# The first score work of each next layer is moved between the last MLP step's products, in a fused four-layer transformer kernel

## The chip, the cores and the metric

The kernel runs on one core of one Trainium2 chip. The metric is the device time of one execution in microseconds (us); lower is better. A core has TensorE (PE in the rows; PEld is its weight load), VectorE (DVE), ScalarE (ACT), GpSimd (POOL) and SyncE, whose queue (SPq) issues most DMAs.

## What is computed

An input x of 32 sequences x 128 tokens x 144 channels goes through four conditioned transformer layers. Each layer normalises, modulates with a shift and a scale made from a condition vector, does attention with 16 heads of 9 dimensions, and an MLP with 576 hidden units:

```python
h = modulate(norm(x), shift_msa, scale_msa)
q, k, v = split(h @ w_qkv + b_qkv)            # 16 heads of 9
# layer 2 alone: q = q / |q| * 3 * qg, k = k / |k| * 3 * kg, each head by itself
attn = softmax(q @ k.T * 9 ** -0.5)
x = x + gate_msa * (attn @ v @ w_proj + b_proj)
h = modulate(norm(x), shift_mlp, scale_mlp)
# layer 0: four experts, top two of them weighted per token; layers 1 to 3: one MLP
x = x + gate_mlp * (gelu(h @ w1 + b1) @ w2 + b2)
```

Layers 0 to 2 attend within a sequence. Layer 3 groups tokens in another way (a head-by-head product for each token), which the kernel gets by masked score tiles of the same size.

## The kernel before, in words

**Tiling.** Everything stays in SBUF as 32 sequences, in 8 groups of 4. Sequence group n of layer l has the number n = 8l + g (so 16 is the first of layer 2, 17 the second). An attention phase works through 64 units of 8 heads of one sequence; U is the running number of a unit over all layers, so group n starts at U = 8n and layer l at U = 64l. An MLP phase has 8 steps g, one for each group.

**One unit of attention.** TensorE makes the scores for the maximum (L650, `scores_for_max`) into banks 0 and 1; VectorE takes the negated maxima (L1546, `head_max`). For two units at a time TensorE turns these (L657, `turn_max`) and VectorE copies them out (L1553, `max_out`, tile mT). Then TensorE makes the scores again, transposed and with the maximum taken off (L668 and L672, `scores`), ScalarE takes the exponential (L1235, `weights`), and TensorE multiplies with V (L684, `weigh`). Outputs are turned back (L692) and divided on VectorE (`normed`, L1562 and L1564). `scores_for_max` runs AHEAD = 5 units before `weigh`.

**How q and k come to be.** While group n is attended to, q and k of group n+2 are projected in three pieces m = 0, 1, 2 (`q_and_k`). ScalarE rounds a piece to bfloat16 (`part1`, L1195), VectorE makes the rest (`rest1`, L1496, tile res), GpSimd makes two further parts (`parts23`, L1962 and L1964). SyncE writes them to DRAM (L417, layer 3: L420) and reads them back in another layout in 12 DMAs (L447, `read_parts`). The first `scores_for_max` of a group waits for all 12. In unit u = 3 of each group TensorE does that of the next group. In layer 2, q and k are first made by token (L613), their squares summed (`head_sums`, L1505), the factor 1/|q| found by three Newton rounds (`head_factors`, L1515 to L1528), and VectorE multiplies (`head_norms`, L1537); then TensorE transposes the pieces (L597). There the three pieces are finished in units u = 3, 4 and 5.

**The rows of the next phases.** Each group is normalised before it is turned (`stats`, `factor`, `normalise` on VectorE: L1472 and L1474, tile xn; `copies` on GpSimd: L1957, tile xr). In the MLP of layer l the groups 0, 1, 2 of the next layer are made ready, too; group 3 of the next layer (numbers k = 35 for layer 2 and 51 for layer 3) is normalised in step 7.

**What sets the order.** Each engine runs one hand-written list; semaphores alone tie the lists together. An engine that waits does nothing behind the wait, and the same holds for SyncE's queue. At a layer's start, `start_layer` on TensorE did five `scores_for_max`, two `turn_max` and the first `scores` in a row (for layer 3 the first five, and for layer 1 as well, stood in the last MLP step already). TensorE's first expert product (L960) waited on one semaphore, `q_w1`, for all four experts' weights.

## Time and profile before

| | |
|---|---|
| median of 3 runs | 1554.76 us (1547.8 to 1559.91) |
| the profiled execution | 1548.05 us, of which the span from first to last instruction is 1546.1 us |
| granted TensorE clock over the span | 0.964 of full |
| layer 0: attention, MLP | 64 to 246 us, 246 to 582 us |
| layer 1: attention, MLP | 583 to 757 us, 758 to 869 us |
| layer 2: attention, MLP | 880 to 1100 us, 1100 to 1219 us |
| layer 3: attention, MLP | 1221 to 1450 us, 1451 to 1546 us |

The span is counted from the first instruction, and every time in the rows is on that scale. The durations and positions are those of the one profiled execution.

### The profile page before, as it was taken

Reading aid. Unit: us, or ns where it says so; the run is one execution under the profiler, and the core shown is the slowest. Engines: PE = TensorE matmul, PEld = TensorE weight load, DVE = VectorE, ACT = ScalarE, POOL = GpSimd, SP = SyncE. Lnnn points to the kernel's source line nnn. Section 1 sums busy time; section 2 is a strip of 40 time slices with the busy share of each in tenths; the row PEclk is TensorE's granted clock in tenths of the full one; section 3 lists DMA queues with packets and bytes.
Section 4 is the critical chain, followed back from the end, with each engine's and each line's share of the span. In section 5 each row is a group of like instructions: output and inputs, shape, how many; then the busy total and the mean of one; then the engine's idle time right before and its main releaser. Section 6 shows DMA issues by size and latency. Waiting matters only on the chain. (4 is left out here: it accounts for less than half of the span.)

```text
span 1546.1 us, 41104 instructions
## 1 busy us (share of the span) xinstructions
PE 1410.9 (91%) x16016; PEld 1055.9 (68%) x16016; DVE 1036.5 (67%) x2601; ACT 779.5 (50%) x1287; POOL 541.6 (35%) x739
## 2 busy tenths in 40 slices
PE   5799988999999998999999688877999799998998
PEld 2377676777777776777777566666776577776776
DVE  4698885666776677888447689897355466665342
ACT  2377664333323336676555366665544365555543
POOL 3355542211131304554323324433335134343222
PEclk9799999999999999999999899999999799999999
DMA  4765631111122123554001333453207576774011
GB/s 129 161 151 155 148 95 52 51 44 44 36 70 70 33 73 87 144 146 120 20 29 46 105 94 92 110 129 86 45 24 108 90 109 114 132 131 93 25 54 47
DMA packets 209129, 134.94 MB, mean 87 GB/s; under 512 B 142461, under 2 KB 191320, under 8 KB 202730
## 3 DMA queue, kind: packets, MB, share of 16 engines
q1 hardware_dynamic: 188978, 129.74, 35.3%
q10 hardware_dynamic: 19960, 2.57, 1.2%
q8 instruction: 130, 2.13, 0.6%
q14 instruction: 61, 0.50, 0.1%
HBM read 98.24 MB, written 33.24 MB: 85 GB/s over the span
## 5 line engine op out<-in xcount | busy, mean ns | idle before, releaser
L1546 DVE TENSOR_REDUCE negm<-banks 128x8 bf16<-128x1024 f32 x256 | 311.0, 1215 | 81.4 <-PE banks L650 79.6
L1235 ACT ACTIVATE prob<-banks 128x1024 f32<-128x1024 f32 x256 | 262.5, 1025 | 191.9 <-PE banks L672 191.1
L1363 ACT ACTIVATE hid<-banks 128x512 f32<-128x512 f32 x144 | 86.0, 597 | 220.3 <-PE banks L961 220.2
L1977 POOL TENSOR_TENSOR X<-X,gx 128x288 f32<-128x288 f32 x128 | 104.1, 826 | 255.0 <-DVE gx L1576 253.2
L977 PEld LDWEIGHTS banks<-wfc,hid 128*128 128x128 f32 x1152 | 156.6, 190 | 29.9 <-issue 20.3
L668 PE MATMUL banks<-qk 54*128 54x128 bf16 (+1 forms) x2048 | 168.7, 236 | 5.3 <-ACT prob L1235 5.0
L672 PE MATMUL banks<-mT,identb 64*128 64x128 bf16 x2048 | 165.7, 225 | 0.9 <-issue 0.9
L977 PE MATMUL banks<-wfc,hid 128*128 128x144 f32 x1152 | 161.1, 286 | 0.0
L650 PE MATMUL banks<-qk 54*128 54x128 bf16 (+1 forms) x2048 | 122.9, 241 | 39.6 <-DVE negm L1546 24.9
L960 PE MATMUL banks<-hT,wfc 128*128 128x512 f32 x288 | 149.6, 601 | 2.4 <-DMA wfc<-in_L_cond_w 2.4
L684 PE MATMUL banks<-prob,V 128*32 128x128 f32 x4096 | 143.5, 282 | 0.0
L1745 DVE TENSOR_TENSOR hid<-hid,qk 128x512 f32<-128x512 f32 x128 | 89.2, 697 | 80.4 <-ACT hid L1363 69.5
L1483 DVE TENSOR_SCALAR hmod<-banks,modr 64x128 f32<-64x128 f32 x256 | 86.8, 396 | 78.2 <-PE banks L583 77.9
L1962 POOL CAST parts<-res 96x512 bf16<-96x512 f32 x96 | 59.0, 615 | 218.7 <-DVE res L1496 217.8
L1388 ACT ACTIVATE hid<-banks 128x512 f32<-128x512 f32 (+1 forms) x120 | 71.1, 596 | 123.0 <-PE banks L951 122.2
L997 PE MATMUL banks<-wfc,hid 128*128 128x144 f32 (+1 forms) x960 | 128.6, 291 | 0.2 <-DVE gx L1576 0.2
L997 PEld LDWEIGHTS banks<-wfc,hid 128*128 128x128 f32 (+1 forms) x960 | 124.4, 194 | 3.9 <-issue 2.7
L650 PEld LDWEIGHTS banks<-qk 54*128 54x128 bf16 (+1 forms) x2048 | 70.0, 102 | 82.0 <-DVE negm L1546 38.2
L950 PE MATMUL banks<-hT,wfc 128*128 128x512 f32 x240 | 124.3, 599 | 0.0
L684 PEld LDWEIGHTS banks<-prob,V 128*32 128x32 f32 x4096 | 107.1, 112 | 16.9 <-issue 6.4
L1178 ACT ACTIVATE hT<-banks,modm 128x128 f32<-128x128 f32 x256 | 99.1, 454 | 34.7 <-PE banks L576 34.6
L961 PE MATMUL banks<-hr,rfc 66*128 66x512 f32 x144 | 115.4, 802 | 0.0
(169 smaller groups left out, 2777.0 us busy)
## 6 DMA issues: line engine op xcount, KB each, us to landing
qk<-qk_scr SPq DMA_DIRECT2D x96, 216.0 KB
gbuf<-gate_scr SPq DMA_DIRECT2D x64, 288.0 KB, 4.5
qk_scr<-parts SPq DMA_DIRECT2D x48, 288.0 KB, 2.8
qk<-qk_scr SPq DMA_DIRECT2D x96, 144.0 KB
qk<-cw_scr SPq DMA_DIRECT2D x8, 1024.0 KB, 4.9
qk_scr<-parts SPq DMA_DIRECT2D x48, 144.0 KB, 2.4
qk<-qk_scr SPq DMA_DIRECT2D x96, 72.0 KB
qk<-tok_scr SPq DMA_DIRECT2D x32, 216.0 KB
```

Source lines behind the costliest of these rows:

```text
L650: mm = pe.matmul(bank[s][:, T * i:T * i + T], operand(l, 0, n, U, s, i), operand(l, 1, n, U, s, i), start=True, stop=True)
L668: pe.matmul(bank[2 + s][:, at], operand(l, 1, n, U, s, i), operand(l, 0, n, U, s, i), start=True, stop=False)
L672: mm = pe.matmul(bank[2 + s][:, at], one_hot(half, 64 * s + 4 * (u % 2) + i, [64, T]), mT[half, u // 2, :], start=False, stop=True)
L684: mm = pe.matmul(bank[4][32 * i:32 * i + 32, T * (2 * s + u % 2):T * (2 * s + u % 2 + 1)], V[:, n % 3, u // 2, VS * h:VS * h + 32], prob[: ...
L950: pe.matmul(bank[2 + i % 2][:], wfc1_t[:, at:at + 128], hT[:, h, :], start=True, stop=False)
L960: pe.matmul(bank[2 + i % 2][:], w, hT[:, h, :], start=True, stop=False)
L961: pe.matmul(bank[2 + i % 2][:], x, hr[:, h, :], start=False, stop=True).then_inc(s_fc1, 1)
L977: mm = pe.matmul(bank[4 + b // 2][:, C * (b % 2):C * (b % 2) + C], hid[:, i % KT, T * b:T * b + T], wfc2[:, e - (t == KT - 1), t, :], star ...
L997: mm = pe.matmul(bank[4 + q][:, C * (b % 2):C * (b % 2) + C], hid[0:rows, t, T * b:T * b + T], wfc2[0:rows, k, t, :], start=(t == 0), stop ...
L1235: act.activation(prob[:, 2 * (U % 3):2 * (U % 3) + 2, :], pairs[1][:], ACT.Exp, scale=scale).then_inc(a_exp, 1)
L1546: dve.tensor_reduce(negm[:, u // 2, :, 4 * (u % 2):4 * (u % 2) + 4], pairs[0][:].rearrange("q s (h k) -> q s h k", k=T), AX.X, ALU.max, ne ...
L1977: pool.tensor_tensor(x, x, gx[:, q, :, :], ALU.add).then_inc(g_x, 1)
```

## The change

Five things change, all by where a step stands in a list, with the same mathematics.

1. **Layer starts.** For layers 1, 2 and 3 the first `turn_max` and the first `scores` move from the layer's start into step 7 of the MLP before, between its products; for layer 2 the first five `scores_for_max` and `head_max` go there too. For layer 3 the first `scores_for_max` stands ahead of the last step's transposes, and so it does for layer 2. VectorE's steps are put in to match: `stats` of group 3 moves to the head of step 7, and its `normalise` moves too (layer 3: to the head of step 7; layer 2: to behind the fifth maximum, the last step of the phase).
2. **Exponential's table.** ScalarE runs a one-element exponential (`exp_table`) behind the last GELU of layers 0, 1 and 2, so that the table is loaded there.
3. **Expert weights.** Each expert's weights have a semaphore, and TensorE waits for an expert's own before its first tile of step 0.
4. **GpSimd scales q and k** of layer 2: `scale_heads` (2 small and 2 large instructions a group) for VectorE's 8 instructions of `head_norms`. Rounds 2 and 3 of `head_factors` now stand together in unit 0.
5. In the expert MLP the last `normed` stands ahead of the first `weighted`.

```diff
-        q_w1 = sem("q_w1")
+        q_w1 = [sem(f"q_w1{e}") for e in range(E)]
@@ tensor: attention, mlp
-                start_layer(l)
+                    if l == 2:
+                        pe.wait_ge(a_qt, CR + 4 * 3)
+                    turn_max(32 * l + 1)
-                    pe.wait_ge(q_w1, 16 * 3 * E)
+                    if g == 0 and t == 0:
+                        pe.wait_ge(q_w1[e], 16 * 3)
+                    if l in (1, 2) and g == 7 and t == 4:
+                        if l == 2:
+                            pe.wait_ge(q_mask, 16 * 12)
+                        scores_for_max(l + 1, U0)
                     if t == 4 and g > 0 and turned_mlp(l, g):
                         turn(turned_mlp(l, g)[0], *before(g))
+                    if l in (1, 2) and g == 7:
                         if b == 0:
+                            scores_for_max(l + 1, U0 + 1)
+                        if b == l % 2 + 1:
+                            first_turn()
+                            scores_for_max(l + 1, U0 + 2)
+                        if b == l % 2 + 2:
+                            scores(l + 1, U0)
+                    if l == 1 and g == 7 and b == 3:
+                        scores_for_max(2, U0 + 3)
+                        if g == 7 and j == NT - 3:
+                            first_turn()
+                        if g == 7 and j == NT - 2:
+                            pe.wait_ge(a_gelu, CR + fc1_base[1])
+                            scores(1, U0)
@@ vector: attention, mlp
-                        if l == 2 and 0 < g < 6 and u <= 1:
-                            head_factors(n + 2, False, (u + 2,))
-                        if l == 2 and g < 6 and 1 <= u <= 2:
-                            head_norms(n + 2, u - 1)
+                        if l == 2 and g < 6 and u == 0:
+                            head_factors(n + 2, False, (2, 3))
                 if l == 1:
+                    head_max(2, U0 + 3)
                     rest1(N + 1, 1, 7)
                     rest1(N + 1, 2, 6)
+                    head_max(2, U0 + 4)
+                    normalise(16 * l + 19)
                     head_sums(N + 2)
-                    head_factors(N + 2)
@@ gpsimd: new, called in units 0 of layer 2's attention and in steps 4 and 6 of layer 1's MLP
+            def scale_heads(n):
+                r = n - 16
+                qs, _ = by_token(n)
+                pool.wait_ge(d_nw, CR + 12 * (r + 1))
+                for side in range(2):
+                    x = rs[:, :, H * side:H * side + H]
+                    pool.tensor_scalar(x, x, gains[:, 2 + side:3 + side], None, ALU.mult).then_inc(g_rg, 1)
+                pool.wait_ge(a_qt, CR + 4 * (r + 1))
+                for side in range(2):
+                    pool.wait_ge(g_rg, CR + 2 * r + side + 1)
+                    v = qs[:, :, C * side:C * side + C].rearrange("t b (d h) -> t b d h", d=D)
+                    pool.tensor_tensor(v, v, rs[:, :, H * side:H * side + H].unsqueeze(2).to_broadcast([T, G, D, H]),
+                                       ALU.mult).then_inc(g_qn, 1)
@@ scalar
+            def exp_table():
+                act.activation(warm[:], mhalf[:, 0:1], ACT.Exp)
```

GpSimd's list at the end of layer 1's MLP is not changed but for the scaling: `copies` of group k = 35 stands ahead of pieces 1 and 2 of group 17 there.

VectorE, from the first statistics of step 7 of layer 1's MLP to layer 2's start. `L1472` is `normalise`, `L1496` `rest1` of group 17, `L1505` the head sums of group 18. Before:

```order
L1455 BN_STATS stat<-X 128x6 x4
L1460 BN_AGGR mv<-stat 128x2 x4
L1496 TENSOR_TENSOR res<-banks,parts 96x512
L1472 TENSOR_SCALAR xn<-X,rstd 128x144 x4
L1576 TENSOR_TENSOR gx<-banks,gbuf 128x288 x2
L1496 TENSOR_TENSOR res<-banks,parts 96x512 x2
L1505 TENSOR_REDUCE ss<-hid 128x32 x4
```

And changed, where `L1569` is `head_max`, `L1530` `rest1`, `L1599` the gate and `L1506` `normalise`:

```order
L1523 SCALAR_TENSOR_TENSOR hr<-hhi,masks,hmod 64x512
L1576 COPY mT<-banks 128x128
L1569 TENSOR_REDUCE negm<-banks 128x2x4
L1530 TENSOR_TENSOR res<-banks,parts 96x512
L1599 TENSOR_TENSOR gx<-banks,gbuf 128x288 x2
L1569 TENSOR_REDUCE negm<-banks 128x2x4
L1530 TENSOR_TENSOR res<-banks,parts 96x512 x2
L1569 TENSOR_REDUCE negm<-banks 128x2x4
L1506 TENSOR_SCALAR xn<-X,rstd 128x144 x4
L1539 TENSOR_REDUCE ss<-hid 128x32 x4
```

The normalisation stood ahead of the last two pieces of group 17 and now stands behind them and behind two more maxima.

GpSimd at the same place, changed (before it is the same but for the line numbers and the two rows that scale, which aren't there). `L1992` copies the row just named, `L2026` adds to X, `L1997` and `L1999` are `parts23` of group 17, and `L2008` and `L2013` scale group 18:

```order
L1992 COPY xr<-xn 128x256
L2026 TENSOR_TENSOR X<-X,gx 128x288 x2
L1997 CAST parts<-res 96x512
L1999 TENSOR_TENSOR parts<-res,parts 96x512
L1997 CAST parts<-res 96x512
L1999 TENSOR_TENSOR parts<-res,parts 96x512
L2008 TENSOR_SCALAR rs<-rs,gains 128x4x16 x2
L2013 TENSOR_TENSOR hid<-hid,rs 128x4x144 x2
```

The parts of group 17 stand behind the copy, so behind the normalisation.

TensorE in step 7 of layer 1's MLP. Before, with `L997` the second products and `L597` the transposes of group 17's q and k:

```order
L951 MATMUL banks<-hr,rfc 128x512
L576 MATMUL banks<-ident,xn 128x128 x4
L583 MATMUL banks<-ident,xr 64x128 x4
L997 MATMUL banks<-wfc,hid 128x144 x20
L597 MATMUL banks<-ident,prob 96x128 x12
```

And changed, where `L651` is `scores_for_max`, `L999` the second products, `L658` `turn_max`, `L669` and `L673` `scores`:

```order
L951 MATMUL banks<-hr,rfc 128x512
L651 MATMUL banks<-qk 128x128 x8
L577 MATMUL banks<-ident,xn 128x128 x4
L584 MATMUL banks<-ident,xr 64x128 x4
L999 MATMUL banks<-wfc,hid 128x144 x5
L651 MATMUL banks<-qk 128x128 x8
L999 MATMUL banks<-wfc,hid 128x144 x10
L658 MATMUL banks<-identb,negm 128x128
L651 MATMUL banks<-qk 128x128 x8
L999 MATMUL banks<-wfc,hid 128x144 x5
L669 MATMUL banks<-qk 128x128 x2
```

The first scores of group 16 now stand ahead of everything else that step 7 has left.

## Rows read from the trace of the kernel before

**Rows 1.** The page's first part: engine, busy us (share of the span), instructions.

```profile
PE 1410.9 (91%) x16016; PEld 1055.9 (68%) x16016; DVE 1036.5 (67%) x2601; ACT 779.5 (50%) x1287; POOL 541.6 (35%) x739
```

**Rows 2.** Stretches: bounds, length, busy us by engine (instructions), clock, DMA share, GB/s.

```profile
578.00:592.00 14.00, 10.20 (x140) 7.84 (x140) 8.56 (x17) 4.95 (x5) 2.08 (x3) 0.88 0.01 1
863.00:903.00 40.00, 24.99 (x264) 19.48 (x264) 28.03 (x62) 15.12 (x29) 10.91 (x17) 0.74 0.27 75
1202.00:1237.00 35.00, 26.24 (x233) 18.75 (x233) 19.11 (x39) 11.31 (x18) 6.72 (x9) 0.73 0.49 87
```

**Rows 3.** Timeline, start of layer 0's MLP: start us, us, instruction xcount [idle before <-releaser].

```profile
246.71 1.13 PE L960 MATMUL banks<-hT,wfc 128*128 128x512 f32 x2 [2.39 <-DMA wfc<-in_L_cond_w]
...
256.40 1.14 PE L977 MATMUL banks<-wfc,hid 128*128 128x144 f32 x8
...
252.81 0.69 DVE L1745 TENSOR_TENSOR hid<-hid,qk 128x512 f32<-128x512 f32 x1 [8.03 <-DMA qk<-cw_scr]
```

**Rows 4.** Timeline, from layer 0's last products to layer 1's start.

```profile
578.36 3.21 PE L977 MATMUL banks<-wfc,hid 128*128 128x144 f32 x24
...
587.40 1.06 PE L583 MATMUL banks<-ident,xr 128*64 128x128 f32 x4
...
584.06 1.28 ACT L1235 ACT_TABLE_LOAD   x1 [6.31 <-PE banks L672]
```

**Rows 5.** Timeline of SyncE's queue: the 12 reads of groups 16, 17, 19, 20, 23.

```profile
849.87 4.23 SPq L447 DMA_DIRECT2D qk<-qk_scr  x12
...
881.23 4.64 SPq L447 DMA_DIRECT2D qk<-qk_scr  x12
...
941.49 4.36 SPq L447 DMA_DIRECT2D qk<-qk_scr  x12
...
970.88 4.45 SPq L447 DMA_DIRECT2D qk<-qk_scr  x12
...
1056.60 4.43 SPq L447 DMA_DIRECT2D qk<-qk_scr  x12
```

**Rows 6.** Timeline of TensorE: first `scores_for_max` of groups 17, 19, 20, 23.

```profile
902.84 0.40 PE L650 MATMUL banks<-qk 54*128 54x128 bf16 x8
...
956.76 0.40 PE L650 MATMUL banks<-qk 54*128 54x128 bf16 x8 [0.70 <-DMA qk<-qk_scr]
...
986.77 0.61 PE L650 MATMUL banks<-qk 54*128 54x128 bf16 x8 [1.21 <-DMA qk<-qk_scr]
...
1071.05 0.61 PE L650 MATMUL banks<-qk 54*128 54x128 bf16 x8 [2.79 <-DMA qk<-qk_scr]
```

**Rows 7.** Timeline, steps 6 and 7 of layer 1's MLP.

```profile
862.78 0.63 PE L576 MATMUL banks<-ident,xn 128*128 128x128 f32 x4 [1.27 <-DVE xn L1472]
...
868.59 1.04 PE L597 MATMUL banks<-ident,prob 128*96 128x128 f32 x8
...
859.49 2.32 DVE L1537 SCALAR_TENSOR_TENSOR prob<-prob,gains,rs 128x144 f32<-128x144 f32 x8
...
870.46 2.15 DVE L1472 TENSOR_SCALAR xn<-X,rstd 128x144 f32<-128x144 f32 x4
...
873.27 1.27 DVE L1496 TENSOR_TENSOR res<-banks,parts 96x512 f32<-96x512 f32 x2
...
877.41 1.16 POOL L1964 TENSOR_TENSOR parts<-res,parts 96x512 bf16<-96x512 f32 x1
```

**Rows 8.** Timeline around layer 3's start.

```profile
1213.20 0.64 PE L650 MATMUL banks<-qk 62*128 62x128 bf16 x8 [3.63 <-DVE negm L1546]
...
1236.91 0.64 PE L650 MATMUL banks<-qk 62*128 62x128 bf16 x8
...
1208.49 5.18 SPq L447 DMA_DIRECT2D qk<-tok_scr  x12
```

**Rows 9.** Lines L1977 and L1948 of GpSimd: ns min/median/max, first and last start, form.

```profile
L1977 POOL TENSOR_TENSOR X<-X,gx x128: 787/795/1285, 101.3 to 1542.5; 128x288 f32<-128x288 f32 x128
...
L1948 POOL TENSOR_SCALAR xn<-X,mv,rstd x100: 842/852/1427, 53.5 to 1451.8; 128x144 f32<-128x144 f32 x100
```

More of the change, by code:

```diff
@@ L593, in q_and_k @@
                 if l == 2:
[L594 removed]
+                    pe.wait_ge(g_qn, CR + 2 * (n - 16) + (2 if m else 1))
                     qs, _ = by_token(n)
@@ L1619, in attention @@
                     dve.wait_ge(d_gate, CR + 2 * m0)
-                for U in range(64 * l, 64 * l + AHEAD):
-                    if l in (0, 2):
-                        head_max(l, U)
-                    if U % 2 == 0 and U > 64 * l:
+                for U in range(AHEAD if l == 0 else 0):
+                    head_max(l, U)
+                    if U in (2, 4):
                         max_out(U // 2 - 1)
+                if l:
+                    max_out(32 * l + 1)
+                if l == 2:
+                    head_factors(n0 + 2, True, (1,))
                 for g in range(8):
@@ L1815, in expert_step @@
                         gated(m0 + g, q, acc[:, 2 * q:2 * q + 2, :])
-                def first_maxima():
-                    for U in range(UNITS * N, UNITS * N + AHEAD):
-                        head_max(l + 1, U)
+                U0 = UNITS * N
                 for g in range(8):
@@ L1831, in mlp @@
                         rest1(N, 2, 6)
+                    if l in (1, 2) and g == 7:
+                        stats(16 * l + 19)
+                        if l == 2:
+                            normalise(16 * l + 19)
+                        head_max(l + 1, U0)
                     for k in turned_mlp(l, g):
                         mod_rem(k, 7)
+                        if l in (1, 2) and g == 7:
+                            head_max(l + 1, U0 + 1)
                         split_rem(k)
-                    for k in prepared_mlp(l, g):
+                    if l in (1, 2) and g == 7:
+                        max_out(U0 // 2)
+                        head_max(l + 1, U0 + 2)
+                    for k in prepared_mlp(l, g) if g < 7 else []:
                         stats(k)
@@ L1842, in mlp @@
                         head_factors(N + (g - 4) // 2)
-                        for side in range(2):
-                            head_norms(N + (g - 4) // 2, side)
                     if l == 1 and g in (5, 7):
                         rest1(N + (g - 5) // 2, 0, 6)
-                    for k in prepared_mlp(l, g):
+                    for k in prepared_mlp(l, g) if g < 7 else []:
                         normalise(k)
@@ L2029, in mlp @@
                         factor(k)
+                    if l == 1 and g in (4, 6):
+                        scale_heads(N + (g - 4) // 2)
                     if g == 0:
```

67 lines of the change are left out of this document (35 added, 32 removed).

## The prediction, made blind

> **What bounds the kernel now.** I read the page's busy shares first: TensorE is busy 91% of the span, VectorE 67% [rows 1]. A change that removes no product can only take from TensorE's idle 9% and from the stretches in which its clock is down. The stretches at the layer boundaries, read next, show where that is [rows 2]: 14 us at the boundary of layers 0 and 1 hold 3.8 us of TensorE idle at a clock of 0.88, 40 us at that of layers 1 and 2 hold 15.0 us at 0.74, 35 us at that of 2 and 3 hold 8.8 us at 0.73. Those are what the first change can reach.
>
> Then the attention phases, by the first score product of each group on TensorE and SyncE's queue beside it. In layer 2 the product waits for the reads of q and k and for nothing else: 0.70, 1.21 and 2.79 us at groups 19, 20 and 23 [rows 6]. The reads' first issue and the product belong together: 941.49 to 956.76, 970.88 to 986.77, 1056.60 to 1071.05, so 15.3, 15.9 and 14.5 us [rows 5, 6]. From the product of one group to the next group's reads pass 14.1 us more (956.76 to 970.88). The two make up the whole period, 30.0 us from group 19 to 20. So attention turns in a ring: product in unit 3, pieces of q and k in units 3 to 5, parts, write, read, next group's product in unit 3. What is taken off elsewhere is given back as a wait at that product, and what makes the ring's first turn late makes the phase late.
>
> **Start of layer 0's MLP.** TensorE starts at 246.71 after 2.39 us of waiting for weights [rows 3]. With expert 0's own semaphore it can start at 244.8, when VectorE has set the row of ones. Two things then stand in the way of the first second-product, at 256.40 before: the divided output, which waited behind VectorE's 8.03 us on the experts' weights per token and now stands ahead of them, and those weights themselves, there at 252.81 as before. VectorE needs 0.69 us: the product can start at about 253.5. Gain 256.40 - 253.5 = **2.9**. If its wait of some 2 us brings the clock down, 1.5.
>
> **Layers 0 to 1.** Before: three second products from 578.36 to 581.6, a turn, mT, the first scores, then 1.28 us of table load at 584.06 and an exponential of 1.02, and the first transposes at 587.40 at half clock (1.06 for what takes 0.60 at full) [rows 4]. After: the turn and the scores (0.8 in all) stand between the products, whose last ends at 582.4; the exponential runs beside it, its table having been loaded behind the last GELU (577.8); a maximum's scores and the second unit's scores take 1.2; the transposes wait for VectorE's gates (two sums, two gates: 1.8) until 583.9. That is 3.5 us early, and 0.6 more comes from the clock: **4.1**, between 3.5 and the 5 that idle and clock leave room for [rows 2].
>
> **Layers 1 to 2.** This is the boundary with most idle time and, I think, where the change loses. Three steps:
>
> (a) Step 4 of the MLP: GpSimd's scaling stands ahead of the copies for which step 5's transposes wait. A large instruction has 576 elements a partition; by the rate of the nearest row, 795 ns for 288 [rows 9], it takes 1.6, with the two small ones 4.1 us a group; by the dearer rate of L1948, 852 ns for 144, it takes 3.4 and the group 7.7. I take 4.1, since L1977 is the same operation on two tensors. VectorE was done with its 2.32 us [rows 7] sooner. TensorE loses 0.9, and all of group 16 comes so much later.
>
> (b) The first scores of group 16 now stand ahead of step 7's transposes. They need group 16's reads, issued at 849.87 [rows 5]: with 0.9 and 14.5 to 15.9 us, there at 865.3 to 866.7. TensorE arrives at 862. So a wait of 4 us, at 862.78 one of 1.27 before [rows 7], and behind it wait the transposes, the four second products and group 17's q and k. With half clock behind the wait the products end at 875.2 and group 17's first piece is transposed at 876.5, where before that was at 868.59.
>
> (c) From there: piece 0 through ScalarE and VectorE 1.2; gates 0.8; a maximum 1.2; pieces 1 and 2, 1.3; a maximum 1.2; and only then group 35's normalisation, 0.9: 883.3, where before it stood at 870.46, ahead of those pieces at 873.27 [rows 7]. GpSimd's list has that group's copy ahead of pieces 1 and 2, so: copy 0.5, X 1.6, two pieces 3.8, end 889.2 (before 877.41 + 1.16 = 878.6). The reads follow 2.7 later as before (878.6 to 881.23), at 891.9, and TensorE's first product of group 17 14.5 later: 906. Before it was at 902.84 [rows 6]. All that the reordering gains on the other path (VectorE would be ready at 896.6, 6 us early) is lost in that wait of 9 us. Taking 3.2 late, and 1.6 for half clock behind the wait: **-4.8**.
>
> **Layer 2's attention.** VectorE loses 8 instructions a group, 2.32 us [rows 7] in six groups, in units 1 and 2. They lie beside the reads' flight, not in the ring: behind unit 3's product each piece waits for TensorE. The cover for GpSimd's 4.1 us is that same flight; the scaled q must be there by unit 2. By the row, 14 us and not 2.3. I take **+1** for the six groups, for waits better spread and so less half clock (0.61 for what takes 0.40 at 986.77 and 1071.05 [rows 6]), with -5 and +5 as bounds: 1.6 us for up to three groups either way.
>
> VectorE's normalisation took 2.15 us for four at 870.46, while GpSimd worked, and 0.9 elsewhere [rows 7]. The Trainium skill, SBUF — State Buffer, section Who interferes with whom, says that GpSimd and VectorE share a port pair by an exclusive lock, which speaks against moving this work: by it, up to 1.6 of the 2.3 us a group come back as blocked VectorE time. That 2.15 agrees; the sum does not need it.
>
> **Layers 2 to 3.** The reads of group 24 are in long before and the masks, too, so the first scores don't wait. `stats` and `normalise` of group 51 go to a place where VectorE was idle. The wait of 3.63 us on the first maximum at 1213.20 goes [rows 8], and so do the five maxima in a row, the two turns and the table load. Step by step: products end at 1213.6, fifth scores 1214.0, VectorE's last maximum and gates 1216.1, second unit's scores 1216.3, transposes 1216.8, first piece 1217.9 at full clock. The first product of group 25, at 1236.91 before, comes 7 us later, at 1225. Its reads were issued at 1208.49 [rows 8] and with 14.5 are in at 1223. Gain 1236.9 - 1225.1 = **11.8**; 8.8 of it is the idle in the stretch, the rest the clock [rows 2]. If the reads take 15.9 or more, less: 9. The ring then carries it on.
>
> **Sum.** 2.9 + 4.1 - 4.8 + 1 + 11.8 = 15.0. From the profiled execution's 1548.05 that gives 1533; it lies 6.7 under the median. From the median, 1554.8 - 15.0 = **1540**.
>
> **Rivals.** (A) The reads of group 17 are not late, as the reordering would have it: VectorE's normalisation finds an earlier place because the pieces wait longer than it, or the reads of group 16 come sooner. Then that boundary gives +6 instead of -4.8: 26 us, 1529. For it: 15.0 us of idle stand there; against it: both lists have the order of (c) fixed. (B) Layer 2's period is VectorE's, not the ring's: its share of busy time there is high, and 2.3 us in six groups would be 14 more, 1526. Against it: the waits for reads at groups 19, 20, 23. (C), on the other side: GpSimd's large instruction takes 8 us. From 5.1 us each it decides: the second must be done 10 us after the factors, before unit 3's transposes. Then each of six groups is 5.7 us later, 34 in all, with 5 more at step 4: 15 - 39, so 24 slower, 1579. Against it: the dearest row gives 3.4. (D) The loss at layers 1 to 2 is deeper: reads of 17 at 909 and half clock in three more groups: -9 and -5, layer 3 +9, the rest 5: 0, so 1555.
>
> **How the numbers follow.** Forecast 0.55; A 0.15; B 0.10; D 0.13; C 0.03; the rest 0.04 is anything slower. The forecast's own bounds are gains of 8 to 21. The range from 1528 to 1552 leaves out C, most of D and a part of B. About 1% (15.5 us) is what a measurement of this kernel can tell from no change; the forecast lies on that line, so it is split in halves: faster by over 1%: 0.27 + 0.15 + 0.10 = 0.52; within 1%: 0.28 + 0.13 + 0.02 = 0.43; slower 0.05.
>
> **What the changed profile would show.** Right: TensorE's first expert product some 2 us sooner; no table load between scores and exponential; a wait for reads of some 4 us ahead of step 7's transposes in layer 1 and one of some 9 us at group 17's first product; unit-3 waits in layer 2 still on reads, period 27 to 30 us; GpSimd's large instruction at 1.6 us; layer 3's group 25 product 12 us nearer to the end of layer 2's products. Wrong: if group 17's product waits for VectorE, A holds; if layer 2's groups take 25 us, B; if TensorE waits for GpSimd's scaled q in each group, C.

## The result, and the profile after

The changed kernel takes 1538.51 us (median of 11 executions, 1537.55 to 1541.85), the kernel before 1552.84 (11 executions beside it, 1547.49 to 1559.91): ratio 0.9911, 95% interval 0.9894 to 0.9927, 14 us faster. The profiled execution took 1537.86, its span is 1536.0. The kernel before's profiled execution took 1548.05, near the fast end of its own runs, so the two traces differ by 10 us and not by 14.

The page's first part answers to [rows 1]. VectorE has 64 instructions fewer and GpSimd 32 more; TensorE's work is the same.

```profile
PE 1409.2 (92%) x16016; PEld 1058.1 (69%) x16016; DVE 1028.2 (67%) x2537; ACT 781.9 (51%) x1290; POOL 569.8 (37%) x771
```

The stretches of [rows 2], same bounds, in the changed kernel:

```profile
578.00:592.00 14.00, 12.97 (x211) 8.71 (x210) 11.55 (x23) 8.29 (x11) 6.24 (x8) 1.00 0.15 41
863.00:903.00 40.00, 25.46 (x270) 20.45 (x266) 26.79 (x51) 15.50 (x30) 14.18 (x19) 0.80 0.27 75
1202.00:1237.00 35.00, 33.07 (x337) 23.82 (x336) 21.25 (x36) 16.38 (x27) 8.12 (x10) 0.85 0.73 114
```

At the first boundary TensorE's 3.8 us of idle are 1.0 and the clock is full. At the third, 8.8 us of idle are 1.9. At the second, idle is 14.5 us where it was 15.0: nothing was won there.

The timeline of the second boundary shows why. It answers to [rows 5 to 7]:

```profile
862.76 0.40 PE L651 MATMUL banks<-qk 54*128 54x128 bf16 x8 [3.96 <-DMA qk<-qk_scr]
863.09 0.90 PE L577 MATMUL banks<-ident,xn 128*128 128x128 f32 x4
...
864.64 2.44 PE L999 MATMUL banks<-wfc,hid 128*128 128x144 f32 x10
...
872.38 0.64 PE L598 MATMUL banks<-ident,prob 128*96 128x128 f32 x4
...
876.15 1.27 DVE L1530 TENSOR_TENSOR res<-banks,parts 96x512 f32<-96x512 f32 x2
...
878.48 0.89 DVE L1506 TENSOR_SCALAR xn<-X,rstd 128x144 f32<-128x144 f32 x4
...
879.50 0.40 POOL L1992 COPY xr<-xn 128x256 f32<-128x256 f32 x1 [3.21 <-issue]
...
879.97 1.55 POOL L2026 TENSOR_TENSOR X<-X,gx 128x288 f32<-128x288 f32 x2
...
881.59 0.61 POOL L1997 CAST parts<-res 96x512 bf16<-96x512 f32 x1
...
887.99 4.24 SPq L448 DMA_DIRECT2D qk<-qk_scr  x12
...
902.30 0.61 PE L651 MATMUL banks<-qk 54*128 54x128 bf16 x8 [6.67 <-DMA qk<-qk_scr]
```

TensorE waits 3.96 us for group 16's reads, with step 7's transposes behind it, and the ten products after them run at half clock (2.44 for what takes 1.39 at full). The rests of group 17's pieces 1 and 2 are done at 877.4, but GpSimd, whose list has the copy and X first, idles 3.21 us for the normalisation at 878.48 and comes to them at 881.59. So group 17's reads are issued at 887.99 (881.23 before), and its product waits 6.67 us.

To see where time comes from, I read the first `scores_for_max` of a group from each trace and took the distances. The columns are the time of group 8's, then the us from one group's to another's, and from group 31's to the last instruction. The third row is a second profile of the changed kernel, the rows below it are the experiments. What lies ahead of group 7 is in no column: group 7's product stands at 213.6 before and between 211.2 and 216.9 in the thirteen others.

```
                        at 8    7-8   8-9   9-15  15-17  17-23  23-25  25-31  31-end
before                 567.6  354.1  28.8  133.5  172.9  168.2  165.9  177.9   131.2
changed                565.3  349.5  24.5  135.0  177.6  173.0  156.7  173.3   130.7
changed, again (e11)   562.9  351.7  24.5  136.5  175.2  168.5  155.6  179.2   131.7
e9  start undone       570.5  355.2  29.0  134.8  176.7  169.4  156.5  178.8   131.6
e6  2-3 undone         566.7  349.8  24.5  133.3  175.7  172.9  166.3  176.5   132.2
e2  VectorE scales     564.0  349.7  24.5  134.0  171.5  174.1  155.8  176.3   131.4
e1  factors            564.1  349.8  24.5  134.0  177.4  170.8  156.7  177.4   131.9
e8  cut scaling        566.8  351.6  24.5  135.2  177.4  168.1  156.3  179.1   131.8
e3  normalise early    566.9  351.7  24.5  133.9  172.7  174.6  155.8  176.4   131.3
e4  turn first         566.6  351.5  24.5  134.3  171.5  171.5  156.3  179.1   131.8
e5  e1+e3+e4           566.7  351.9  24.5  134.2  169.6  169.8  156.0  179.1   131.8
e12 e5 again           561.6  350.0  24.5  136.9  169.5  169.6  156.4  176.1   131.7
e10 e5, loads later    567.1  350.3  24.5  136.5  169.1  167.9  158.4  175.0   132.2
e7  short reads        565.7  349.8  24.5  134.6  174.6  159.7  154.9  168.6   130.8
```

### The profile page after: what moved, and what is told of

Its sections match the earlier page's. It is cut to its first block, busy times and chain, and to the rows that moved or that the text cites. A ratio compares the mean times of both kernels' runs of the same rounds, so it can differ in the third digit from the quotient of the medians.

```text
span 1536.0 us, 41073 instructions
## 1 busy us (share of the span) xinstructions
PE 1409.2 (92%) x16016; PEld 1058.1 (69%) x16016; DVE 1028.2 (67%) x2537; ACT 781.9 (51%) x1290; POOL 569.8 (37%) x771
## 4 chain that ended last, share of the span: by engine, by line
PE 66%; DMA 11%; DVE 9%; issue 4%; SPq 4%; POOL 3%; ACT 2%; POOLq 0%; DVEq 0%; ACTq 0%
PE banks L979 9%; PE banks L962 8%; PE banks L999 7%; DMA qk<-qk_scr 7%; PE banks L950 6%; PE banks L685 5%; DVE negm L1569 4%; PE banks L651 4%; PE banks L669 3%; SPq L448 3%; PE banks L607 3%; PE banks L716 2%; PE banks L963 2%; PE banks L673 2%; PE banks L693 2%
## 5 line engine op out<-in xcount | busy, mean ns | idle before, releaser
L1569 DVE TENSOR_REDUCE negm<-banks 128x8 bf16<-128x1024 f32 x256 | 311.1, 1215 | 90.7 <-PE banks L651 88.7
L2026 POOL TENSOR_TENSOR X<-X,gx 128x288 f32<-128x288 f32 x128 | 104.3, 827 | 267.8 <-DVE gx L1599 266.1
L979 PEld LDWEIGHTS banks<-wfc,hid 128*128 128x128 f32 x1152 | 156.7, 190 | 31.9 <-issue 20.1
L669 PE MATMUL banks<-qk 54*128 54x128 bf16 (+1 forms) x2048 | 169.5, 236 | 5.4 <-issue 3.3
L673 PE MATMUL banks<-mT,identb 64*128 64x128 bf16 x2048 | 166.2, 225 | 0.0
L651 PE MATMUL banks<-qk 54*128 54x128 bf16 (+1 forms) x2048 | 123.1, 242 | 38.0 <-DMA qk<-qk_scr 18.9
L999 PE MATMUL banks<-wfc,hid 128*128 128x144 f32 (+1 forms) x960 | 130.5, 293 | 0.0
L999 PEld LDWEIGHTS banks<-wfc,hid 128*128 128x128 f32 (+1 forms) x960 | 126.1, 196 | 3.9 <-issue 2.7
L1997 POOL CAST parts<-res 96x512 bf16<-96x512 f32 x96 | 59.1, 616 | 180.4 <-DVE res L1530 179.5
L651 PEld LDWEIGHTS banks<-qk 54*128 54x128 bf16 (+1 forms) x2048 | 70.2, 102 | 80.9 <-issue 47.5
L669 PEld LDWEIGHTS banks<-qk 54*128 54x128 bf16 (+1 forms) x2048 | 109.6, 101 | 8.6 <-issue 3.9
```

The lines of the kernel that those rows point to most:

```text
L651: mm = pe.matmul(bank[s][:, T * i:T * i + T], operand(l, 0, n, U, s, i), operand(l, 1, n, U, s, i), start=True, stop=True)
L669: pe.matmul(bank[2 + s][:, at], operand(l, 1, n, U, s, i), operand(l, 0, n, U, s, i), start=True, stop=False)
L673: mm = pe.matmul(bank[2 + s][:, at], one_hot(half, 64 * s + 4 * (u % 2) + i, [64, T]), mT[half, u // 2, :], start=False, stop=True)
L979: mm = pe.matmul(bank[4 + b // 2][:, C * (b % 2):C * (b % 2) + C], hid[:, i % KT, T * b:T * b + T], wfc2[:, e - (t == KT - 1), t, :], star ...
L999: mm = pe.matmul(bank[4 + q][:, C * (b % 2):C * (b % 2) + C], hid[0:rows, t, T * b:T * b + T], wfc2[0:rows, k, t, :], start=(t == 0), stop ...
L1569: dve.tensor_reduce(negm[:, u // 2, :, 4 * (u % 2):4 * (u % 2) + 4], pairs[0][:].rearrange("q s (h k) -> q s h k", k=T), AX.X, ALU.max, ne ...
```

## The experiments

All edits are shown abridged; `...` marks what is left out.

### e1: the factors' second round earlier

```diff
-    if l == 2 and g < 6 and u == 0:  head_factors(n + 2, False, (2, 3))
+    if l == 2 and g < 6 and u == 0:  head_factors(n + 2, False, (3,))
...
-    if l == 2 and g < 5 and u == 7:  head_factors(n + 3, True, (1,))
+    if l == 2 and g < 5 and u == 7:  head_factors(n + 3, True, (1, 2))
```

> The changed kernel with the second round of the heads' factors moved back from unit 0 of a group in layer 2 to unit 7 of the group before; unit 0 keeps the third alone. The profile after has group 17's first product at 902.3 and group 23's at 1075.3, 173.0 us for six groups, where before it was 168.2. Theory 1 (VectorE's list in units 0 and 1 sets the pace): three instructions of 0.33 us leave the way of hmod in each of six groups, so 173.0 becomes 168 to 170, and TensorE's wait on hmod ahead of the transposition of On (5.7 us in the six groups) falls under 2. Theory 2 (the reads' flight sets it, as my prediction has it): the 1.0 us a group come back as waits for reads, 173.0 stays within 1.

Measured: 1538.67 us, ratio to before 0.991 (0.9886 to 0.9934), as the changed kernel. Groups 17 to 23 took 170.8 us, between the two theories (168 to 170, and 173 within 1); and the changed kernel's second profile has 168.5 for the same stretch without the edit. Inconclusive: the stretch varies more by itself than the edit could give.

### e2: q and k scaled by VectorE again

```diff
-    scale_heads(n + 2)                       # GpSimd, at the group's start
...
+    if l == 2 and g < 6 and u <= 1:      head_factors(n + 2, False, (u + 2,))
+    if l == 2 and g < 6 and 1 <= u <= 2: head_norms(n + 2, u - 1)
```

> The changed kernel with q and k scaled by VectorE again, in the places of the kernel before; the factors' rounds 2 and 3 again in units 0 and 1. Theory 1 (GpSimd's large instruction holds VectorE's split of the rest, which takes 1.66 us in layer 2 and 0.74 elsewhere): that split is back at 0.74 in all groups, the six groups of layer 2 are back from 173.0 to 168 to 169 us, and step 4 gives 0.9 more: 4 to 6 us faster than the changed kernel. Theory 2 (the 2.3 us a group of VectorE's work count in full): six groups take 173 + 14 = 187. Theory 3 (the reads' ring alone): 173 stays within 1, the kernel is as fast as the changed one.

Measured: 1539.16 us, 0.9919 (0.9889 to 0.9949): the same as the changed kernel, as theory 3 says of the total. VectorE's split of the rest is back at 0.74 us, but layer 2's six groups took 174.1 and not 168; nor did they take 187. So neither VectorE's 2.3 us a group nor the hold-up costs the layer anything that stands out of its scatter (168.5 to 174.6 where its lists are those of the changed kernel). The gain that I did not expect is at 15 to 17: 171.5. Reckoned from group 15's product, TensorE comes to the wait for group 16's reads 1.3 us later than in the changed kernel's second profile and the reads are in 0.8 sooner: the wait is 2.47 us, and behind it the clock holds:

```profile
856.60 0.40 PE L651 MATMUL banks<-qk 54*128 54x128 bf16 x8 [2.47 <-DMA qk<-qk_scr]
...
856.93 0.66 PE L577 MATMUL banks<-ident,xn 128*128 128x128 f32 x4
...
857.86 1.39 PE L999 MATMUL banks<-wfc,hid 128*128 128x144 f32 x10
```

The changed kernel's second profile has a wait of 4.61 at the same place, and the same transposes and products at half clock:

```profile
858.80 0.61 PE L651 MATMUL banks<-qk 54*128 54x128 bf16 x8 [4.61 <-DMA qk<-qk_scr]
...
859.35 1.11 PE L577 MATMUL banks<-ident,xn 128*128 128x128 f32 x4
...
861.11 2.60 PE L999 MATMUL banks<-wfc,hid 128*128 128x144 f32 x10
```

### e3: input 35 normalised ahead of the gates

```diff
-    for k in prepared_mlp(l, g) if g < 7 else []:            normalise(k)
+    for k in prepared_mlp(l, g) if g < 7 or l == 1 else []:  normalise(k)
...
     head_max(2, U0 + 4)
-    normalise(16 * l + 19)
```

> The changed kernel with the normalisation of the second layer 2 group's fourth input (35) back ahead of the gates in step 7 of layer 1's MLP. Theory 1 (my step c: GpSimd's copy and its two additions to X stand ahead of group 17's pieces 1 and 2 and wait for that normalisation): they are done by 878.3 and not 881.5, the reads of group 17 are issued at 884.7 and not at 888.0, and its first product stands at 899.0 to 899.5 and not at 902.3; the span is 3 us shorter. Theory 2 (the two additions wait for the gates, which move 0.9 later): no more than 1 us. Theory 3: the gain is there at group 17 and gone by group 23.

Measured: 1539.79 us, 0.9913 (0.988 to 0.9946). Groups 15 to 17 took 172.7 us; 175.2 and 177.6 in the two profiles of the changed kernel. Group 17's product stands at 897.95 and its wait is 3.33 us, half of what it was. So step (c) of the prediction is the cause of some 2.5 to 5 us there; the clock at step 4, of which e4 tells, fell in e3 as in the changed kernel's first profile, and against that one the gain is 4.9. But groups 17 to 23 took 174.6, and the end came at the same 1536: theory 3 in this profile, and the median shows no gain either.

### e4: step 7's transposes ahead of group 16's scores

```diff
-    if l in (1, 2) and g == 7 and t == 4:   # ahead of step 7's transposes
+    if l == 2 and g == 7 and t == 4:
         scores_for_max(l + 1, U0)
...
+    if l == 1 and b < 2:                    # behind the first second-products
+        scores_for_max(2, U0 + b)
```

On VectorE both maxima stand behind `split_rem`.

> The changed kernel with group 16's first two scores for the maximum, at the boundary of layers 1 and 2, behind the transposes of step 7 and behind the first two of its second products. Theory 1 (my step b: TensorE's wait of 3.96 us for group 16's reads holds the transposes): transposes at 859.6 and not at 863.1, group 17's first piece transposed at 869 and not at 872.4, group 17's product at 899 and not at 902.3, granted clock of 863 to 903 over 0.80, span 3 to 4 us shorter. Theory 2: the wait only moves behind the transposes, to the scores ahead of the second products' second half, and the end stays within 1 us.

Measured: 1536.03 us, 0.9893 (0.9866 to 0.992). Group 16's product no longer waits, group 17's stands at 896.91 (899 expected), 171.5 us from group 15's; its own wait is 6.92 us, no shorter than before the edit. A part of the gain is not the edit's: at step 4 of the MLP, where the two kernels are alike, the changed kernel's products ran at half clock and e4's did not. The windows from one step's first product to the next, of the changed kernel and then of e4 (the clock is the third figure from the end), show it:

```profile
825.50:833.40 7.90, 7.90 (x53) 7.90 (x54) 4.22 (x12) 2.77 (x6) 1.54 (x2) 0.78 0.12 39
```

```profile
825.30:831.55 6.25, 6.25 (x52) 6.25 (x53) 4.24 (x11) 2.76 (x6) 1.56 (x3) 1.00 0.14 50
```

Ahead of both lies the same wait:

```profile
824.79 0.60 PE L584 MATMUL banks<-ident,xr 128*64 128x128 f32 x4 [1.79 <-POOL xr L1992]
```

```profile
824.65 0.60 PE L584 MATMUL banks<-ident,xr 128*64 128x128 f32 x4 [1.81 <-POOL xr L1996]
```

Twelve profiles have GpSimd's scaling ahead of that wait (all but before and e2). The clock fell in five of them (changed, e1, e3, e8, e9), one of these being e8, where the wait was 2.61 us. It held in the changed kernel's second profile; against that one, e4 gains 3.7 us from group 15 to 17 and not 6.1.

### e6: the boundary of layers 2 and 3 undone

```diff
+    if l == 3:                              # at the layer's start, as before
+        pe.wait_ge(d_hm, CR + 4 * (NTH[m0 + 2] + 1))
+        start_layer(l)
...
-    if l < 3 and g == 7:                    # ScalarE
+    if l == 1 and g == 7:
         exp_table()
...
-    head_max(3, U0 + 3); head_max(3, U0 + 4)
+    for U in range(U0, U0 + AHEAD): head_max(3, U)   # five in a row
```

> The changed kernel with the boundary of layers 2 and 3 as in the kernel before (five maxima in a row, the turn, table load and exponential at layer 3's start). Theory 1 (my term of 11.8 us): group 23 to group 25's first product takes 165 to 166 us (156.67 in the changed kernel, 165.85 before) and the kernel is 9 to 12 us slower than the changed one. Theory 2 (layer 3's ring of reads sets its later groups whatever the start was): the 9 us are there at group 25 and only 3 to 6 us at the end.

Measured: 1549.2 us, 0.9974 (0.9955 to 0.9993): by the medians 10.7 us over the changed kernel, by the ratios to before 9.8. Groups 23 to 25 took 166.3, as before the change; all other profiles with the new order have 154.9 to 158.4. The wait on the first maximum is back, at the clock of 0.67:

```profile
1215.10 0.64 PE L651 MATMUL banks<-qk 62*128 62x128 bf16 x8 [3.39 <-DVE negm L1576]
```

```profile
1204.00:1239.00 35.00, 26.57 (x229) 19.22 (x228) 18.97 (x39) 11.00 (x17) 6.24 (x9) 0.67 0.51 88
```

Theory 1: this one boundary carries most of the change's gain, and layer 3 gave none of it back that its scatter (173.3 to 179.2) would show.

### e7: the reads cut to one row

```diff
+    if 18 <= n < 24 or n >= 27:
+        src, dst = src[0:1], dst[0:1]
     sp.dma_start(dst, src).then_inc(q_r[r][s], 16)
```

> The changed kernel with the 12 reads of q and k cut to one row each in groups 18 to 23 and 27 to 31, so those groups work on stale data: the output is not the reference's, and only the times of the groups are read from it. Theory 1 (the ring: product, pieces, parts, write, read, next product sets the groups of layers 2 and 3 at 28 to 30 us): the flight of 14 to 16 us falls to 6 to 8 and the groups to 23 to 25 us, until TensorE's or VectorE's own work sets them; no wait for reads is left. Theory 2 (the ring hardly binds, VectorE or TensorE set 28 us): the groups stay at 27 to 28.

Measured: span 1513.4 us, 22.6 less (one execution). Six groups of layer 2 took 159.7 us. The first comes 27.38 us behind group 17, the next four stand 27.05 us apart (953.80, 980.84, 1007.89, for instance), and group 23 comes 24.10 behind group 22. SyncE still issues each group's reads 12.5 us behind the product before, but nothing waits for them; what TensorE waits for is VectorE's divided output (14 times, 11.8 us in the 120 below):

```profile
966.30 3.48 SPq L450 DMA_DIRECT2D qk<-qk_scr  x12
```

```profile
980.68 0.23 PE L660 MATMUL banks<-identb,negm 128*128 128x128 bf16 x1 [1.08 <-DVE On L1589]
980.84 0.34 PE L653 MATMUL banks<-qk 54*128 54x128 bf16 x6
```

The busy times in 120 us of layer 2 and 140 of layer 3 (TensorE, its loads, VectorE, ScalarE, GpSimd):

```profile
930.00:1050.00 120.00, 100.60 (x1827) 82.61 (x1824) 109.40 (x242) 81.92 (x137) 70.93 (x105) 1.00 0.20 58
1240.00:1380.00 140.00, 139.64 (x1974) 104.61 (x1974) 93.32 (x193) 85.07 (x128) 59.20 (x78) 0.98 0.56 77
```

So the ring binds, but by little: without it 27.05 us a group is the floor in layer 2, with VectorE busy in 109.4 of 120 us and TensorE waiting for its outputs, and the ring makes 28 to 30 of it where a read is late. That is not every group: in the changed kernel's second profile, with whole reads, groups 19 and 22 come 27.05 and 27.04 us behind the ones before, with no wait, as the ring at its best (reads 12.5 us behind the product, used 14.5 later) gives the same 27. The steadiest loss is at group 23, which waits 3.5 to 4.5 us in every changed kernel with whole reads and stands 27.7 to 30.0 behind group 22 instead of 24.1. In layer 3 TensorE itself is the bound without reads. Theory 1 had the mechanism and missed the floor (23 to 25); theory 2 had the floor and denied the ring.

### e8: GpSimd's scaling cut into short instructions

```diff
-    pool.tensor_tensor(v, v, factor, ALU.mult)                # 128x576, one a side
+    for b in range(G): pool.tensor_tensor(v_b, v_b, factor_b, ALU.mult)   # 128x144, four a side
```

> The changed kernel with each of GpSimd's two large scaling instructions (576 elements a partition, 1.40 us) cut into four of 144. Theory 1 (VectorE's instruction stands until the GpSimd instruction that runs beside it ends): VectorE's split of the rest in layer 2's groups, 1.66 us mean there and 0.74 elsewhere, falls to 1.0 to 1.3, and the four normalisations beside it in step 4, 3.37 us, fall under 2.5. Theory 2 (the two engines share a rate, whatever the length of an instruction): both stay. By either the span is within 2 us of the changed kernel's, since neither is in the ring.

Measured: 1538.54 us, 0.9894 (0.9856 to 0.9932), as the changed kernel. VectorE's split of the rest in layer 2 (groups of lines, 885 to 1060 us; the changed kernel, then e8, then e2, where GpSimd scales nothing):

```profile
L1523 DVE SCALAR_TENSOR_TENSOR hr<-hhi,masks,hmod 64x512 fp32r<-64x512 f32 x6 | 10.8, 1793 | 0.3 <-ACT hhi L1213 0.3
```

```profile
L1523 DVE SCALAR_TENSOR_TENSOR hr<-hhi,masks,hmod 64x512 fp32r<-64x512 f32 x6 | 5.5, 912 | 0.0
```

```profile
L1523 DVE SCALAR_TENSOR_TENSOR hr<-hhi,masks,hmod 64x512 fp32r<-64x512 f32 x6 | 4.4, 736 | 0.0
```

1793, 912 and 736 ns: the shorter the instruction beside it, the shorter the hold-up. Step 4's four normalisations took 3.37 us and then 1.88 (0.90 where GpSimd is idle). Theory 1 holds. What the cutting costs is GpSimd's own time, 3.61 us for eight and not 2.77 for two.

### e9: the start of layer 0's MLP and the boundary of layers 0 and 1 undone

```diff
-    if g == 0 and t == 0:
-        pe.wait_ge(q_w1[e], 16 * 3)
...
+    for e in range(E):                      # ahead of the first product
+        pe.wait_ge(q_w1[e], 16 * 3)
...
-    if g == 7 and j == NT - 3: first_turn()
-    if g == 7 and j == NT - 2: scores(1, U0)
+    if l == 1: start_layer(l)
```

The divided output stands behind `weighted` again, and the table load at layer 1's start.

> The changed kernel with its first part undone: TensorE waits for all four experts' weights before layer 0's first expert product, the divided output stands behind the weighted hidden layer again, and layer 1's turn, first scores, table load and exponential stand at the layer's start. Theory 1 (my terms of 2.9 and 4.1 us): group 8's first product 2 to 3 us later against group 7's, and group 8 to group 9's 28.8 us as in the kernel before (24.5 in the changed one), the kernel 6 to 7 us slower than the changed one. Theory 2 (as with layer 3's ring, what stands early is given back later): layers 2 and 3 take it back and the end is 2 to 4 us later.

Measured: 1546.94 us, 0.9946 (0.9917 to 0.9974), 6.3 us over the changed kernel measured beside it (1540.67, e11; the two kernels' executions, 1538.7 to 1552.3 and 1533.6 to 1554.6, overlap widely, so the stretches of the profile are the better witness). Groups 8 to 9 took 29.0 us, not 24.5, in all other changed kernels alike. From group 7 to group 8 it took 355.2 us; 354.1 before; 349.5 to 351.9, 350.6 on average, in the twelve others: 4.6 us, more than the 2 to 3 expected, with TensorE's wait for all four experts' weights at 3.12 us here (2.39 before). Theory 1: both terms are there, and by the medians they are there at the end.

### e11 and e12: the changed kernel and e5 once more, and e5 itself

e5 is e1, e3 and e4 together.

> The changed kernel with three edits together: the early normalisation of input 35, the transposes of step 7 ahead of group 16's first scores, and the second round of the heads' factors in unit 7. Alone, the first two left group 17's first product at 897.95 and 896.91 (902.30 in the changed kernel). Theory 1 (the two delays are in series): group 17's product 3 us earlier again, at 894, and its wait for reads down from 6.9 to under 4 us; layer 2's pace stays near 29 us a group, since its ring sets it; span 1531, 1.2 to 1.5% under the kernel before. Theory 2 (layer 3's ring gives back what layers 1 to 2 won): group 25's first product is 9 us earlier than in the changed kernel, and the span 4 us or less.

> The changed kernel once more, unedited. Layer 3's groups 25 to 31 took 173.3 us in its profile and 176.3 to 179.1 in the profiles of five kernels with edits elsewhere. Theory 1 (a chance of the clock behind waits): now 176 to 179 us, with the clock at the fifth step of layer 1's MLP as likely to hold (6.25 us) as to fall (7.9 us). Theory 2 (a property of the changed kernel): 173 to 174 again.

> The kernel of the three edits once more, beside the changed one on the same chip. If its 4 to 5 us under the changed kernel (1533.8 and 1538.5 medians) are its own and not the chip's, it is 3 to 6 us faster again; group 17's product at 895 to 896, layer 3's groups 25 to 31 at 176 to 179 us. If the chip's, within 1.5.

Measured: e5 1533.8 us, 0.9878 (0.9859 to 0.9898); in a later set of runs e12 1532.15, 0.9864 (0.9815 to 0.9912), beside e11, the changed kernel, at 1540.67, 0.9917 (0.9885 to 0.995). The intervals of the ratios touch, but all four executions of e5 (1531.5 to 1534.5) lie under all eleven of the changed kernel's first set (1537.6 to 1541.9), and the repeat has the same sign. So e5 is faster than the changed kernel, by 8.5 us within the later set and by 4.7 across two sets. Group 17's product stands at 895.01, 3 us nearer than by e3 alone (of which 1.65 is e3's clock at step 4) and 2 nearer than by e4 alone, and its wait is 3.76. From group 15 to 17 e5 took 169.6 us and e12 169.5, where the kernel before took 172.9: only with both edits does this boundary gain. In e5's profile it is 11.2 us ahead of the changed kernel at group 25 and 4.3 at the end, theory 2; but e11 shows how to read that: the changed kernel's own layer 3 took 173.3 us in one profile and 179.2 in the other. The first profile had luck in layer 3 (173.3, where the others have 175 to 179) and none in layer 2 (173.0, where its repeat has 168.5).

### e10: weights of the MLP loaded behind the last reads

```diff
-    if l and g == 2:                 load_first(l - 1, q_w2[l - 1])
+    if l and g == (2 if l == 1 else 6): load_first(l - 1, q_w2[l - 1])
...
-    if l and g == 3:                 load_second(l - 1, q_w2[l - 1])
+    if l and g == (3 if l == 1 else 7): load_second(l - 1, q_w2[l - 1])
```

> The kernel of the three edits, with the loads of the MLP's weights in layers 2 and 3 (one of w1 behind the reads of the layer's fifth group, three of w2 and its bias behind those of the sixth) moved behind the layer's last reads. Theory 1 (those loads share the engines with the reads just ahead of them in the ring: the flight of group 20 is 15.6 us, of 21 is 17.1, of 29 is 15.9, and 14.4 to 14.7 elsewhere): they fall to 14.7, groups 20 to 22 are 3 us sooner, group 31 another 1 to 2, span 1528 to 1529 (1531.7). Theory 2 (half clock sets the rest): flights fall, the span by less than 1.5 us. Should the weights come late for the MLP, TensorE waits at its first product and the kernel is slower.

Measured: 1529.19 us, 0.9843 (0.9802 to 0.9885), the fastest median, but its interval overlaps e12's. From reads to product took 14.8 us at group 20 (15.6 and 15.5 in e5 and e12), 15.0 at 29 (15.9 twice), but 16.3 at 21 (17.1 and 16.5); groups 17 to 23 took 167.9 and not 169.7, 25 to 31 175.0 and not 176.1 or 179.1. But groups 23 to 25 took 2 us more, so the loads are felt in the MLP. The direction is theory 1's: most of the fall to 14.7 at groups 20 and 29, a quarter or less of it at 21, 1.8 of 3 us in layer 2. The span (1530.7, between 1531.7 and 1526.2) does not show it, so that it makes the kernel faster is not shown. Why group 21's reads stay long is open.

## Why the prediction was right, and where not

I forecast 1540 by a gain of 15.0; the medians give 14.3, and the two profiled spans 10. Of my three classes the ratio 0.9911 falls in the second, within 1% (0.43), and not in the one I held likeliest, faster by over 1% (0.52). Averaged over the profiles that leave a stretch unedited, the table gives 3.5 (7-8), 4.3 (8-9), -1.3 (9-15), -3.3 (15-17), -3.4 (17-23), 9.6 (23-25), 0.6 (25-31) and -0.4 (to the end): about 9.5, against one profile of the kernel before. The other 5 us have no place: the kernel before's profiled execution lies 4.8 under its median, the changed one's 0.7 under its own. So the right total holds two terms that were off in size, by 2 and by 4 us, and 5 us that no trace places: that it came so near is partly luck. By its steps:

**Start of layer 0's MLP, 2.9.** Right, 3.5 us from group 7 to group 8 (354.1 against 350.6). TensorE starts 1.4 sooner in the first profile, and the first second-product, at 256.40 before, waits for the experts' weights alone:

```profile
245.32 1.13 PE L962 MATMUL banks<-hT,wfc 128*128 128x512 f32 x2 [0.51 <-DVE hid L1481]
...
253.27 2.50 DVE L1769 TENSOR_TENSOR hid<-hid,qk 128x512 f32<-128x512 f32 x4 [4.42 <-DMA qk<-cw_scr]
...
254.02 1.25 PE L979 MATMUL banks<-wfc,hid 128*128 128x144 f32 x8 [1.73 <-DVE hid L1769]
```

**Layers 0 to 1, 4.1.** Measured 4.3 (28.8 against 24.5), the same in all twelve kernels with this part. The table load lies at 575.42, behind the last GELU, and the transposes of [rows 4] run at full clock:

```profile
575.42 1.28 ACT L1256 ACT_TABLE_LOAD   x1
...
581.46 0.63 PE L584 MATMUL banks<-ident,xr 128*64 128x128 f32 x4 [0.43 <-DVE gx L1599]
```

**Layers 1 to 2, -4.8.** Measured -4.7 and -2.3 in the two profiles of the changed kernel, -3.3 on average of the six that leave it unedited. Steps (b) and (c) are as forecast. My times were in the frame of the kernel before; group 15's product is 5.2 us earlier in the changed one (724.73 for 729.94). Less these 5.2: the end of input 35's normalisation was forecast at 878.1 and is at 879.37; reads issued 886.7, are at 887.99; product 900.8, is at 902.30. All three are 1.3 to 1.5 late, 0.9 of it by the clock at step 4, of which step (a) tells below. The waits are 3.96 us (4 forecast) and 6.67 (9). Undoing (b) gave 4 to 6 us (e4), undoing (c) 2.5 to 5 (e3), both together 5.6 and 8.0 against the two profiles (e5); the larger figures of e4 and e5 hold 1.65 us of clock. The boundary was not put back as a whole, as e6 and e9 did with the others. Step (a) is the one that failed. GpSimd's scaling costs what I took (two of 0.44 us and two of 1.41, 3.7; 4.1 forecast), but TensorE's loss of 0.9 behind it is not a fixed price. It waits 1.8 us there, and before it waited 1.51 and 0.17 us at the same place for VectorE:

```profile
828.41 0.63 PE L576 MATMUL banks<-ident,xn 128*128 128x128 f32 x4 [1.51 <-DVE xn L1474]
...
829.72 2.72 PE L997 MATMUL banks<-wfc,hid 128*128 128x144 f32 x20 [0.17 <-DVE gx L1576]
```

So the wait costs 0.1 us more while the clock holds, and 1.65 us on top when it falls, in five profiles of twelve.

**Layer 2's attention, +1.** This term was mis-sized: -4.8 in the first profile, -0.3 in its repeat, -6.4 to -1.2 in four more with the same lists there (e3, e4, e6, e9), -3.4 on average. I gave -5 and +5 as bounds, on the ground that VectorE's relief lies beside the reads' flight. That held: neither giving the work back to VectorE (e2), nor shorter GpSimd instructions (e8), nor earlier factors (e1) moved the stretch beyond its scatter of 6 us. e7 shows the ring that I named as the bound, none to 3 us a group over a floor of 27.05. What I left out is its first turn: group 17's product now comes behind a wait of 6.7 us at half clock (0.61 for 0.40), and SyncE issues group 18's reads 13.3 us behind it (902.30 to 915.60), where before, with no wait, it was 11.5 (902.84 to 914.34).

```profile
915.60 4.23 SPq L448 DMA_DIRECT2D qk<-qk_scr  x12
```

Group by group, in the six profiles with the same lists, group 18 comes 28.2 us behind 17 on average and came 26.1 before: 2.1 of the 3.4. Another 1.4 is at group 23 (28.4, before 27.0); between them gains and losses cancel. Why group 23 waits longer than before is open.

**Layers 2 to 3, 11.8.** Right in mechanism, too large: 9.2 and 10.3 in the two profiles (165.9 against 156.7 and 155.6), 10.7 in e6's median. Group 25's reads came in time, as forecast. The step that was off is the clock behind the last maximum: I had the transposes and the pieces at full clock. In the frame of the changed profile, 4.25 us later at group 23, the transposes were forecast at 1221.1 and start at 1221.90, but group 25's product was forecast at 1229.4 and is at 1231.97. Between them lies half clock: the transposes took 1.06 and not 0.60, the first piece's products 1.91 and not 1.02. The clock had been down once before, ahead of and behind the first scores, and was full again from 1212 to 1217:

```profile
1203.00:1206.50 3.50, 3.50 (x15) 2.00 (x14) 1.06 (x4) 0.88 (x2) 0.40 (x1) 0.74 1.10 129
1206.50:1212.00 5.50, 5.10 (x33) 4.42 (x33) 2.58 (x5) 3.63 (x9) 0.00 (x0) 0.54 0.83 76
1212.00:1217.00 5.00, 5.00 (x61) 4.17 (x55) 3.23 (x4) 1.34 (x3) 0.00 (x0) 1.00 0.35 103
1217.00:1225.00 8.00, 6.83 (x57) 4.25 (x51) 5.80 (x10) 1.88 (x2) 1.55 (x2) 0.80 0.73 157
```

```profile
1211.69 1.28 ACT L1256 ACT_TABLE_LOAD   x1
...
1220.59 0.64 PE L651 MATMUL banks<-qk 62*128 62x128 bf16 x8 [1.17 <-DVE negm L1569]
...
1221.90 1.06 PE L584 MATMUL banks<-ident,xr 128*64 128x128 f32 x4
...
1222.76 1.91 PE L607 MATMUL banks<-hT,wqkv 128*96 128x512 f32 x2
```

**The rivals.** A falls: group 17's reads are late. B falls, since no group came at 25 us and the total did not; but e7 shows how near it was, 27.05 us being what VectorE and TensorE take between them without the ring. C falls, by GpSimd's 1.41 us against 8. D came nearer than its 0.13: in the first profile the boundary gave -4.7 and layer 2 -4.8, together -9.5 against its -14 and my -3.8; only its 1555 is ruled out. Its sum has a slip, "the rest 5" where my own terms for the start and layers 0 to 1 make 7.0.

**The Trainium skill's rule** (SBUF — State Buffer, section Who interferes with whom) is that GpSimd and VectorE hold a shared pair of ports by an exclusive lock. e8 agrees: the hold-up goes with the length of GpSimd's instruction. By it, as I estimated with the time of GpSimd's instruction from [rows 9], up to 1.6 of 2.3 us a group come back as blocked time. At the split of the rest 1.1 came back (1793 against 736 ns), and the time of the kernel did not follow.

## What to carry to other kernels

Work taken from a layer's start into the last products of the layer before pays where the engines it waits for are done: here at the boundary whose inputs had long been read (9 to 10 us), and not at the one whose inputs were in flight, where the moved work waits in front of everything queued behind it (3 us lost, and 3 won once the order behind it was put right). After such a move, look at each in-order list for the instruction that now waits first, and at what stands behind it: two edits of a few lines at that place, which the wait and the idle GpSimd pointed to, took another 4.7 and 8.5 us off in two sets of runs (with e1 in it). Compare more than one profile before a stretch is called slower: the same kernel's layer 2 took 173.0 and 168.5 us, and its layer 3 173.3 and 179.2.

## What the runs showed of the hardware

A VectorE instruction beside a long GpSimd instruction stands until that one ends. In the changed kernel's step 4 four normalisations took 3.37 us (0.90 alone; 1.88 in e8, beside instructions a quarter as long), and the split in layer 2 started at 926.54 ends 0.5 us behind GpSimd's last:

```profile
925.07 2.77 POOL L2013 TENSOR_TENSOR hid<-hid,rs 128x576 f32<-128x576 f32 x2
926.54 1.85 DVE L1523 SCALAR_TENSOR_TENSOR hr<-hhi,masks,hmod 64x512 fp32r<-64x512 f32 x1
```

The same wait of 1.8 us on TensorE in the same program left the clock at 1.00 in one execution, below, and took it to 0.78 in another, the changed kernel's windows under e4, 1.65 us dearer:

```profile
823.02 0.60 PE L584 MATMUL banks<-ident,xr 128*64 128x128 f32 x4 [1.78 <-POOL xr L1992]
```

```profile
823.73:829.98 6.25, 6.25 (x53) 6.25 (x54) 4.24 (x12) 2.77 (x6) 1.54 (x2) 1.00 0.21 50
```

So a term worked out from the trace for half clock behind a short wait has both values in its range.
